# Queries, keys and their stacks made and loaded by halves of the tokens

## Chip, cores and metric

One core of one Trainium2 chip runs the whole program. The metric is the device time of one execution in microseconds (us), as a median over several executions. The chip has one tensor engine (TensorE, PE in the profile; its weight loads stand apart as PEld), a vector engine (VectorE, DVE), a scalar engine (ScalarE, ACT), GpSimd (POOL) and a queue engine (SyncE, SP) that issues nearly all transfers. 16 DMA engines move the data.

## The reference

The input is `x`, 16 images of 192 channels and 32 x 32 pixels. Two layers follow each other:

```python
x = _L0_conv_ref(x, ...)     # norm, q/k/v by 1x1 and 3x3 convolutions, attention over channels, + norm
t = _to_tokens(x)            # 1024 tokens of 192 channels in each image
t = t + _L1_attn_ref(_ln_t(t), W_qkv, W_proj, b_proj)   # 6 heads of 32, causal
t = t + _L1_ffn_ref(_ln_t(t), gate_w, gate_b, w1, b1, w2, b2)   # 4 experts, the best 2 for each token
```

The change lies in the causal token attention:

```python
qkv = jnp.einsum('btc,fc->btf', x, W_qkv)
wei = jnp.einsum('bqhd,bkhd->bhqk', q, k) * scale
wei = jnp.where(causal[None, None], wei, -jnp.inf)
out = jnp.einsum('bhqk,bkhd->bqhd', jax.nn.softmax(wei, axis=-1), v)
```

A query sees only keys that stand at or before it. Queries 0 to 511 so need only keys 0 to 511.

## The kernel before

The program goes through the 16 images one after another (about 171 us each), and then through 67 blocks of 512 routed tokens for the experts. All order is written out by hand: each engine has one list of instructions, and semaphores tie the lists together. A wait holds up everything behind it on its engine.

**The stages of an image.** Convolutions and channel attention come first, then the input of the token attention (`t_sb`, normed to `xhat`). TensorE transposes `xhat` (`norm_transposes`, one call for tokens 0 to 511 and one for the others). ScalarE and VectorE split each transposed half into a high and a low part (`T0`, `T1`, `T2`). `queries_keys(i, n)` then makes 128 rows (32 queries and 32 keys for each of two heads) for one half of the tokens. `f` in `QK_ORDER` is the pair of heads and the second number is the half. There are six such products of five matmuls. ScalarE copies each to `QKh`, and VectorE writes what is left to `QKl`. `values_of_tokens` makes the values.

**The stacks.** A score in near full precision needs three products. Therefore SyncE copies queries and keys inside SBUF into `QS` and `KS`, with 96 rows for each head: high, low, high queries against high, high, low keys. `load_queries` and `load_keys` issue three transfers each. The two heads of pair 0 come first (12 transfers of 128 KB, semaphores `stack_ld[0]` and `[1]`), the four other heads then (12 of 256 KB, `stack_ld[2]` and `[3]`). `QS` lies over `xhat` and over `xhat2`, the rows that GpSimd sends to the experts for the image before. Hence the second set waits for `sent`.

**Units.** The attention of an image has 48 units, `SOFT`: query chunks `qc` of 128 queries by head `h`, chunk by chunk. A unit is a score (`query_scores`), its maximum (VectorE), the exponential (ScalarE), the transposes of the weights (`blocks`), their copy to `PT` (ScalarE or VectorE), and the product with the values once four or two heads are there. Scores run two or three units ahead. `PT` lies over `QKh` and `QKl`, so the first copies of an image wait for all of `stack_ld`.

**What else hangs on SyncE.** Right behind the stacks, SyncE issues the load of the next image (`load_image`, `x_sb`, 768 KB) and zeros for the next expert blocks. VectorE reads that `x_sb` in the middle of the attention: `image_steps` puts `stats(i + 1, 0)` (L803) right behind the copies of unit 6, with a wait for `x_ld`. The further statistics and the norm of the next image follow at fixed units up to unit 27. In the last image, the expert weights (`w_raw`) are loaded in place of the next image, and VectorE splits them from unit 20 on (`split`, L1231 and L1232).

**GpSimd** sends the rows of the image before with 16 indirect transfers (`send`), in two sets of 8, with the two small `token_rstd` between them. It then adds a bias to `t_sb` (L732).

Of the kernel before, what the change touches and what calls it, by code (L numbers as in the profile page):

```python
# [5 lines left out]
F32 = mybir.dt.float32  # L6
# [10 lines left out]
BANK = 512  # L17

def hybrid_block_kernel(nc, x, ln_g, ln_b, conv_w, conv_bias_row, conv_taps, conv_bias, alpha_rows, w_f_t, b_f,  # L20
                        w_qkv_a, w_qkv_b, w_proj, w_proj_t, b_proj, gate_w_a, gate_w_b, gate_b, w1_a, w1_b, b1_t,
                        w2, b2, out):
    B, C, SH, SW = x.shape
    N = SH * SW
    NC = N // P
# [46 lines left out]
    with ExitStack() as ctx:  # L72
# [203 lines left out]
        ring_ld = [sem(f"ring_ld{p}") for p in range(PAIRS)]  # L276
        stack_ld = [sem(f"stack_ld{n}") for n in range(4)]
        x_ld, scr_w, t_st, sent, cleared, dram_written = sems("x_ld scr_w t_st sent cleared dram_written")
# [144 lines left out]

        QK_ORDER = [(0, 0), (1, 0), (0, 1), (2, 0), (1, 1), (2, 1)]
        NQ = len(QK_ORDER)
        QK_FIRST = 1
        COUNT_BANK = 7
# [32 lines left out]
        def _(sp):  # L460
# [64 lines left out]
            for i in range(B):  # L525
                if i:

                    sp.wait_ge(o_sb, NC * i)
                    sp.dma_start(tokens[i - 1], t_sb[:, :, 0:C]).then_inc(t_st, 16)
                def load_queries(j, first, end, signal):  # L530

                    for r, part in enumerate((QKh, QKl, QKh)):
                        sp.dma_start(QS[D * r:D * (r + 1), 2 * first + j:2 * end:2, :].bitcast(F32),
                                      part[D * j:D * (j + 1), first:end, :].bitcast(F32)).then_inc(signal, 16)

                def load_keys(j, first, end, signal):
                    for r, part in enumerate((QKh, QKh, QKl)):
                        sp.dma_start(KS[D * r:D * (r + 1), 2 * first + j:2 * end:2, :].bitcast(F32),
                                      part[64 + D * j:64 + D * (j + 1), first:end, :].bitcast(F32)).then_inc(signal, 16)  # L540

                sp.wait_ge(qk_lo, NQ * i + QK_ORDER.index((0, 1)) + 1)
                for j in range(2):
                    load_queries(j, 0, 1, stack_ld[j])
                    load_keys(j, 0, 1, stack_ld[j])
                sp.wait_ge(qk_lo, NQ * (i + 1))
                if i:

                    sp.wait_ge(sent, SENT * i)
                for j in range(2):  # L550
                    load_queries(j, 1, PAIR_GROUPS, stack_ld[2 + j])
                    load_keys(j, 1, PAIR_GROUPS, stack_ld[2 + j])
                if i + 1 < B:
# [74 lines left out]
        def _(pool):  # L628
# [93 lines left out]
            for i in range(B):  # L722
                unpad_image(pool, i)
                if i:
                    send(i - 1, 0, TPC)
                token_rstd(i, 0)
                token_rstd(i, 1)
                if i:
                    send(i - 1, TPC, NC)

# [9 lines left out]
                token_rstd2(i, 1)  # L740
            send(B - 1, 0, TPC)
            send(B - 1, TPC, NC)

# [46 lines left out]
        def _(dve):  # L790
# [182 lines left out]
            def blocks_out(i, n):  # L973

                qc, h = SOFT[n]
                for t in passage(i).of[n]:
                    eng, count, k0, nb = passage(i).pieces[t]
                    if eng == "dve":
                        dve.wait_ge(pT_ps, blocks_before(i, t))
                        if qc:  # L980
                            dve.wait_ge(pv_ps, 2 * (NC * i + qc - 1) + (1 if h < 4 else 2))
                        elif h == 1:
                            for signal in stack_ld:
                                dve.wait_ge(signal, STACK_LOADS * (i + 1))
# [355 lines left out]
        def _(act):  # L1340
# [48 lines left out]
            def blocks_out(i, n):  # L1389

                qc, h = SOFT[n]
                for t in passage(i).of[n]:
                    eng, count, k0, nb = passage(i).pieces[t]
                    if eng == "act":
                        act.wait_ge(pT_ps, blocks_before(i, t))
                        if qc:
                            act.wait_ge(pv_ps, 2 * (NC * i + qc - 1) + (1 if h < 4 else 2))
                        elif h == 0:
                            for signal in stack_ld:
                                act.wait_ge(signal, STACK_LOADS * (i + 1))  # L1400
# [91 lines left out]
        def _(pe):  # L1492
# [143 lines left out]
            def query_scores(i, n):  # L1636
                qc, h = SOFT[n]
                if n == 0:
                    pe.wait_ge(qk_lo, NQ * (i + 1))
                if n < H:  # L1640
                    pe.wait_ge(stack_ld[h if h < 2 else 2 + h % 2], STACK_LOADS * (i + 1))
                if last_user(n) is not None:
                    pe.wait_ge(exp_sb, NU * i + last_user(n) + 1)
# [299 lines left out]
```

## Time and profile before

| | us |
|---|---|
| median of 3 runs | 4002.49 (3996.62 to 4022.53) |
| the profiled execution, time | 3976.27 |
| its span | 3974.5 |
| TensorE busy | 3252.2 (82%) |
| VectorE busy | 2360.8 (59%) |
| ScalarE busy | 1836.1 (46%) |
| GpSimd busy | 1076.2 (27%) |
| TensorE clock, mean share of full speed | 0.906 |

All durations below come from the profiled execution. Busy shares are means over stages with different limits. So they are read by stage. A row of a timeline gives the start, the duration, the engine and the line of the code, then what was written and read. In square brackets it gives how long the engine stood idle before the row, and what ended that. "SPq" is the issue of a transfer, not the transfer.

### The profile page before, as it was taken

What the parts mean: (1) busy time and instruction counts of PE and PEld (TensorE: products, weight loads), DVE (VectorE), ACT (ScalarE), POOL (GpSimd) and SP (SyncE); (2) the same over time, 40 slices, a digit from 0 to 9 for tenths busy, and PEclk for the clock granted to TensorE, in tenths of its full rate; (3) what the DMA queues carried; (4) which work ended last, traced back from release to release, by engine and by line L of the source; (5) the groups of instructions that cost most, each with busy time, mean ns of one, the idle gap of its engine ahead of it and who ended that gap; (6) DMA issues with size and microseconds to landing.
All of it is one profiled execution on the core that took longest, in us unless ns stands there. A gap on an engine that the chain in (4) does not pass through costs nothing. (4 is left out here: it accounts for less than half of the span.)

```text
span 3974.5 us, 72989 instructions
## 1 busy us (share of the span) xinstructions
PE 3252.2 (82%) x26642; PEld 2468.7 (62%) x26642; DVE 2360.8 (59%) x5963; ACT 1836.1 (46%) x3868; POOL 1076.2 (27%) x1542
## 2 busy tenths in 40 slices
PE   3687887878779787787978779787499999999995
PEld 1465565565545555565565556555488888888884
DVE  3466565666647566465666647566456565656664
ACT  0345263543625435263543526445355555555553
POOL 1011202112020211202112020211336555565543
PEclk9898898988889898898988879897799999999998
DMA  6344353443533335343443533334123433333332
GB/s 148 97 102 122 96 136 89 101 107 87 145 106 94 97 93 132 96 123 92 102 107 88 147 101 94 93 97 116 46 71 106 118 99 109 99 114 94 117 104 86
DMA packets 213097, 414.47 MB, mean 104 GB/s; under 512 B 66799, under 2 KB 130223, under 8 KB 211673
## 3 DMA queue, kind: packets, MB, share of 16 engines
q1 hardware_dynamic: 188169, 359.44, 34.3%
q0 software_dynamic: 24576, 50.36, 4.2%
q8 instruction: 217, 3.56, 0.4%
q14 instruction: 135, 1.11, 0.1%
HBM read 242.86 MB, written 117.71 MB: 91 GB/s over the span
## 5 line engine op out<-in xcount | busy, mean ns | idle before, releaser
L971 DVE TENSOR_REDUCE minus_max<-ps 128x1 f32<-128x128 f32 (+7 forms) x768 | 575.9, 750 | 514.8 <-PE ps L1649 510.0
L1647 PE MATMUL ps<-KS,QS 96*128 96x512 f32 (+3 forms) x1152 | 433.0, 430 | 295.8 <-DMA KS<-QKl 260.1
L1386 ACT ACTIVATE p_sb<-ps,minus_max 128x128 f32<-128x128 f32 (+7 forms) x768 | 567.7, 741 | 115.5 <-DVE minus_max L971 112.0
L1659 PE MATMUL ps<-ident,p_sb 128*128 128x128 f32 x3456 | 555.2, 286 | 31.1 <-ACT p_sb L1386 7.8
L1401 ACT ACTIVATE PT<-ps 128x512 f32<-128x512 f32 (+3 forms) x640 | 340.6, 532 | 395.4 <-PE ps L1659 388.6
L1273 DVE TENSOR_TENSOR g_lo<-g,g_hi 128x512 fp32r<-128x512 f32 x402 | 315.4, 786 | 348.5 <-ACT g_hi L1476 296.9
L1475 ACT ACTIVATE g<-ps,bcur 128x512 f32<-128x512 f32 x402 | 276.6, 688 | 474.3 <-PE ps L1837 373.0
L1853 PE MATMUL ps<-w_all,g_hi 128*128 x1608 | 442.1, 355 | 18.2 <-ACT g_hi L1476 9.2
L706 POOL COPY inverse_wide<-inverse_sums 128x192 f32<-128x192 f32 x128 | 44.7, 349 | 1484.5 <-DVE inverse_sums L993 1484.5
L1647 PEld LDWEIGHTS ps<-KS,QS 96*128 96x128 f32 x1152 | 217.6, 212 | 357.1 <-DMA KS<-QKl 265.7
L1659 PEld LDWEIGHTS ps<-ident,p_sb 128*128 128x128 f32 x3456 | 385.1, 146 | 79.3 <-issue 33.3
L1530 PE MATMUL ps<-ring,wconv 125*32 125x512 f32 (+1 forms) x3072 | 375.2, 630 | 56.7 <-DMA ring<-padded_scratch 56.7
L719 POOL DMA_INDIRECT routed_rows<-xhat,slot x256 | 250.3, 978 | 414.5 <-issue 414.5
L756 POOL CAST cur<-w_all 128x384 fp32r x536 | 289.5, 586 | 244.1 <-PE ps L1837 244.0
L774 POOL DMA_INDIRECT got<-expert_rows,slot x256 | 259.5, 1014 | 201.5 <-issue 133.9
L1858 PE MATMUL ps<-w_all,g_lo 128*128 x1608 | 298.8, 267 | 14.8 <-DVE g_lo L1273 14.3
L1858 PEld LDWEIGHTS ps<-w_all,g_lo 128*128 128x128 f32 x1608 | 288.2, 189 | 29.0 <-DVE g_lo L1273 26.4
L1853 PEld LDWEIGHTS ps<-w_all,g_hi 128*128 128x128 f32 x1608 | 264.9, 192 | 50.7 <-issue 16.7
L985 DVE COPY PT<-ps 128x512 f32<-128x512 f32 (+3 forms) x512 | 246.4, 481 | 71.6 <-PE ps L1659 71.5
L1476 ACT ACTIVATE g_hi<-ps,bcur 128x512 fp32r<-128x512 f32 x402 | 273.7, 681 | 0.0
L1837 PE MATMUL ps<-X_hi,cur 128*128 128x512 f32 x804 | 263.6, 409 | 1.5 <-DVE X L1282 1.5
L1530 PEld LDWEIGHTS ps<-ring,wconv 125*32 125x32 f32 (+1 forms) x3072 | 97.3, 115 | 262.5 <-issue 249.2
(277 smaller groups left out, 5924.4 us busy)
## 6 DMA issues: line engine op xcount, KB each, us to landing
ring<-padded_scratch SPq DMA_DIRECT2D x576, 204.0 KB
routed_rows<-zero_rows SPq DMA_DIRECT2D x67, 384.0 KB, 6.9
xgt<-routed_rows SPq DMA_DIRECT2D x67, 384.0 KB
expert_rows<-y_rows SPq DMA_DIRECT2D x67, 384.0 KB, 2.5
QS<-QKh SPq DMA_DIRECT2D x64, 256.0 KB, 4.6
KS<-QKh SPq DMA_DIRECT2D x64, 256.0 KB, 5.0
padded_scratch<-xpad SPq DMA_DIRECT2D x16, 870.0 KB, 4.6
x_sb<-x SPq DMA_DIRECT2D x16, 768.0 KB, 7.6
```

Of the source, the lines that this page charges most:

```text
L756: g.tensor_copy(cur[r % 2][:, part], w_all[:, bass.ds(expert, 1), part].rearrange("p e f -> p (e f)")).then_inc(cur_sb, 1)
L971: v.tensor_reduce(nmx[:, qc, h:h + 1], score_place(n), AX, ALU.max, negate=True).then_inc(mx_sb, 1)
L1273: v.tensor_tensor(g_lo[:, n % 2, :], g32[:, n % 2, :], g_hi[:, n % 2, :].bitcast(F32), ALU.subtract).then_inc(lo_sb, 1)
L1386: a.activation(p_sb[n % NP][:, 0:P * (qc + 1)], score_place(n), ACT.Exp, bias=nmx[:, qc, h:h + 1], accum_out=ls[:, qc, h:h + 1]).then_inc( ...
L1401: a.activation(PT[h][:, k0:k0 + nb, :], bank(pass_bank(t))[:, 0:P * nb].rearrange("p (k q) -> p k q", q=P), ACT.Copy).then_inc(PT_act, 1)
L1475: a.activation(g32[:, n % 2, :], bank(n % 2), ACT.Gelu, bias=b1)
L1476: a.activation(g_hi[:, n % 2, :], bank(n % 2), ACT.Gelu, bias=b1).then_inc(gelu_sb, 1)
L1530: last = t.matmul(bank(2 * (r % 2) + nh)[W * j:W * (j + 1), :], wconv[s][0:KROWS[s], h, c0:c0 + W], rhs, start=s == 0, stop=s == 1, skip_g ...
L1647: t.matmul(o[:, k0:k0 + keys], QS[0:96, h, P * qc:P * (qc + 1)], KS[0:96, h, k0:k0 + keys], start=True, stop=k0 + keys < P * (qc + 1), ski ...
L1659: last = t.transpose(bank(pass_bank(piece))[:, P * k:P * (k + 1)], p_sb[n % NP][:, P * (k0 + k):P * (k0 + k + 1)], ident[:, :])
L1853: t.matmul(bank(acc_bank(r, tt))[:, 0:2 * C], g_hi[:, n % 2, P * tt:P * (tt + 1)], w2j, start=j == 0, stop=False, skip_group_check=True)
L1858: last = t.matmul(bank(acc_bank(r, tt))[:, 0:C], g_lo[:, n % 2, P * tt:P * (tt + 1)], w2j[:, 0:C], start=False, stop=j == J - 1, skip_grou ...
```

## The change

`QK_ORDER` now makes all three pairs of heads for tokens 0 to 511, then all for the others, and the second transposes stand behind the first three products (`QK_FIRST` is 3). The stacks are loaded in the same order, in 36 transfers where there were 24, with the same bytes in all. There are 12 of 64 KB (pair 0, first half), 12 of 128 KB (the four other heads, first half; keys first), and 12 of 192 KB (all heads, second half). Rows inside a transfer are 2 KB long where they were 4 KB. Two new semaphores, `stack_ld[4]` and `[5]`, tell of the second half. They are waited for at query chunk 4. GpSimd sends 12 transfers ahead of the two `token_rstd` and 4 behind them, where it was 8 and 8.

```diff
-        QK_ORDER = [(0, 0), (1, 0), (0, 1), (2, 0), (1, 1), (2, 1)]
+        QK_ORDER = [(0, 0), (1, 0), (2, 0), (0, 1), (1, 1), (2, 1)]
-        QK_FIRST = 1
+        QK_FIRST = PAIR_GROUPS
...
-                sp.wait_ge(qk_lo, NQ * i + QK_ORDER.index((0, 1)) + 1)
+                sp.wait_ge(qk_lo, NQ * i + 1)
+                sp.wait_ge(lnT_ps, 4 * (i + 1))
                 for j in range(2):
-                    load_queries(j, 0, 1, stack_ld[j])
-                    load_keys(j, 0, 1, stack_ld[j])
-                sp.wait_ge(qk_lo, NQ * (i + 1))
+                    load_queries(j, 0, 1, 0, stack_ld[j])
+                    load_keys(j, 0, 1, 0, stack_ld[j])
+                sp.wait_ge(qk_lo, NQ * i + PAIR_GROUPS)
+                for j in range(2):
+                    load_keys(j, 1, PAIR_GROUPS, 0, stack_ld[2 + j])
                 if i:
 
                     sp.wait_ge(sent, SENT * i)
                 for j in range(2):
-                    load_queries(j, 1, PAIR_GROUPS, stack_ld[2 + j])
-                    load_keys(j, 1, PAIR_GROUPS, stack_ld[2 + j])
+                    load_queries(j, 1, PAIR_GROUPS, 0, stack_ld[2 + j])
+                sp.wait_ge(qk_lo, NQ * (i + 1))
+                for j in range(2):
+                    load_queries(j, 0, PAIR_GROUPS, 1, stack_ld[4 + j])
+                    load_keys(j, 0, PAIR_GROUPS, 1, stack_ld[4 + j])
                 if i + 1 < B:
                     load_image(sp, i + 1)
...
-                    send(i - 1, 0, TPC)
+                    send(i - 1, 0, 6)
...
-                    send(i - 1, TPC, NC)
+                    send(i - 1, 6, NC)
...
-                            for signal in stack_ld:
+                            for signal in stack_ld[0:4]:
+                                dve.wait_ge(signal, STACK_LOADS * (i + 1))
+                        if qc == TPC and h == 0:
+                            for signal in stack_ld[4:6]:
                                 dve.wait_ge(signal, STACK_LOADS * (i + 1))
...
-                if n < H:
+                if qc == 0:
                     pe.wait_ge(stack_ld[h if h < 2 else 2 + h % 2], STACK_LOADS * (i + 1))
+                if qc == TPC and h < 2:
+                    pe.wait_ge(stack_ld[4 + h], STACK_LOADS * (i + 1))
```

**TensorE, between the first product of queries and keys and the first that needs the second half of the tokens.** L1593 (L1602 after) are the transposes of `xhat`. Before:

```order
L1609 MATMUL ps<-T_128,wqkv_b_hi 128x512
L1609 MATMUL ps<-T_128,wqkv_b_lo 128x512
L1593 MATMUL ps<-ident,xhat 128x128 [waits xhat_sb]
L1593 MATMUL ps<-ident,xhat 128x128 x7
L1609 MATMUL ps<-T_hi,wqkv_a_hi 128x512
L1609 MATMUL ps<-T_hi,wqkv_a_lo 128x512
L1609 MATMUL ps<-T_lo,wqkv_a_hi 128x512
L1609 MATMUL ps<-T_128,wqkv_b_hi 128x512
L1609 MATMUL ps<-T_128,wqkv_b_lo 128x512
L1609 MATMUL ps<-T_hi,wqkv_a_hi 128x512 [waits T_hi,T_lo]
```

Now:

```order
L1618 MATMUL ps<-T_128,wqkv_b_hi 128x512
L1618 MATMUL ps<-T_128,wqkv_b_lo 128x512
L1618 MATMUL ps<-T_hi,wqkv_a_hi 128x512
L1618 MATMUL ps<-T_hi,wqkv_a_lo 128x512
L1618 MATMUL ps<-T_lo,wqkv_a_hi 128x512
L1618 MATMUL ps<-T_128,wqkv_b_hi 128x512
L1618 MATMUL ps<-T_128,wqkv_b_lo 128x512
L1602 MATMUL ps<-ident,xhat 128x128 [waits xhat_sb]
L1602 MATMUL ps<-ident,xhat 128x128 x7
L1618 MATMUL ps<-T_hi,wqkv_a_hi 128x512 [waits T_hi,T_lo]
```

The second transposes have moved behind two more products (ten matmuls), and the product that waits for the second half comes right behind them, where one product stood between.

**SyncE, the end of the stack loads and what follows them.** `QS` are the stacked queries, `KS` the stacked keys, the sizes are rows x heads x tokens. Before:

```order
L534 DMA QS<-QKh 32x2x1024
L534 DMA QS<-QKl 32x2x1024
L534 DMA QS<-QKh 32x2x1024
L539 DMA KS<-QKh 32x2x1024 x2
L539 DMA KS<-QKl 32x2x1024
L316 DMA x_sb<-x 96x2x1024 [waits conv_ps]
L333 DMA routed_rows<-zero_rows 16x6144 x4
```

Now:

```order
L533 DMA QS<-QKh 32x3x512 [waits qk_lo]
L533 DMA QS<-QKl 32x3x512
L533 DMA QS<-QKh 32x3x512
L539 DMA KS<-QKh 32x3x512 x2
L539 DMA KS<-QKl 32x3x512
L533 DMA QS<-QKh 32x3x512
L533 DMA QS<-QKl 32x3x512
L533 DMA QS<-QKh 32x3x512
L539 DMA KS<-QKh 32x3x512 x2
L539 DMA KS<-QKl 32x3x512
L316 DMA x_sb<-x 96x2x1024 [waits conv_ps]
L333 DMA routed_rows<-zero_rows 16x6144 x4
```

The last 12 transfers now carry the second half of all six heads. The load of `x_sb` still stands behind all of them, and there are now 36 issues ahead of it since the products, where there were 24.

**GpSimd, the sends of the image before.** Before:

```order
L719 DMA routed_rows<-xhat_136,slot 34304x192 [waits cleared,slot_sb,xhat2_sb]
L719 DMA routed_rows<-xhat_136,slot 34304x192 x7
L694 TENSOR_TENSOR rstd<-rstd,minus_half 128x4 [waits veps] x2
L719 DMA routed_rows<-xhat_136,slot 34304x192 [waits xhat2_sb]
L719 DMA routed_rows<-xhat_136,slot 34304x192 x7
L732 TENSOR_TENSOR t_sb<-t_sb,bproj_bc 128x1568 [waits xhat_sb]
```

Now:

```order
L726 DMA routed_rows<-xhat_136,slot 34304x192 [waits cleared,slot_sb,xhat2_sb]
L726 DMA routed_rows<-xhat_136,slot 34304x192 x11
L701 TENSOR_TENSOR rstd<-rstd,minus_half 128x4 [waits veps] x2
L726 DMA routed_rows<-xhat_136,slot 34304x192 [waits xhat2_sb]
L726 DMA routed_rows<-xhat_136,slot 34304x192 x3
L739 TENSOR_TENSOR t_sb<-t_sb,bproj_bc 128x1568 [waits xhat_sb]
```

Four of the sends have moved ahead of the two `rstd` rows.

## Rows read from the trace of the kernel before

**Rows 1.** Windows: length, busy us (count) of each engine, clock, DMA share, GB/s

```profile
990.50:1014.70 24.20, 8.03 (x57) 7.08 (x55) 2.96 (x7) 5.10 (x15) 5.49 (x3) 0.68 0.90 219
1014.70:1020.20 5.50, 5.48 (x33) 4.26 (x34) 2.98 (x11) 3.46 (x17) 0.00 (x0) 0.53 1.00 364
1020.20:1039.00 18.80, 16.57 (x158) 11.61 (x156) 16.33 (x42) 13.80 (x44) 2.10 (x7) 1.00 0.02 7
```

**Rows 2.** Page, costliest groups: busy, mean ns | idle before, what ended it

```profile
L1647 PE MATMUL ps<-KS,QS 96*128 96x512 f32 (+3 forms) x1152 | 433.0, 430 | 295.8 <-DMA KS<-QKl 260.1
```

**Rows 3.** Timeline, PE: start us, us, operation [idle before <-what ended it]

```profile
1000.06 0.48 PE L1647 MATMUL ps<-KS,QS 96*128 96x128 f32 x1 [2.75 <-DMA KS<-QKl]
...
1007.98 0.47 PE L1647 MATMUL ps<-KS,QS 96*128 96x128 f32 x1 [7.31 <-DMA KS<-QKl]
...
1014.70 0.47 PE L1647 MATMUL ps<-KS,QS 96*128 96x128 f32 x1 [6.12 <-DMA KS<-QKl]
...
1038.94 0.60 PE L1647 MATMUL ps<-KS,QS 96*128 96x512 f32 x2
```

**Rows 4.** Timeline, SP: issues of the sixth image

```profile
990.53 0.54 SPq L534 DMA_DIRECT2D QS<-QKh  x1
...
998.40 0.63 SPq L534 DMA_DIRECT2D QS<-QKh  x1
999.07 0.62 SPq L534 DMA_DIRECT2D QS<-QKl  x1
...
1010.02 0.63 SPq L539 DMA_DIRECT2D KS<-QKl  x1
1010.69 1.21 SPq L316 DMA_DIRECT2D x_sb<-x  x1
```

**Rows 5.** Windows: the DMA share and rate while the stacks are loaded

```profile
1000.00:1005.00 5.00, 0.60 (x2) 0.42 (x2) 0.29 (x1) 0.46 (x2) 0.00 (x0) 0.50 1.00 216
```

**Rows 6.** DMA view, 980:1020 us: KB each, median us to landing

```profile
x_sb<-x SPq DMA_DIRECT2D x1, 768.0 KB, 7.8
QS<-QKh SPq DMA_DIRECT2D x4, 128.0 KB, 2.7
```

**Rows 7.** Timeline, DVE: where the next image's x is first read

```profile
1020.07 0.18 DVE L993 RECIPROCAL inverse_sums<-row_sums 128x6 f32<-128x6 f32 x1
1020.17 0.65 DVE L803 BATCH_NORM_STATS2 pstat<-x_sb 96x6 f32<-96x512 f32 x1
```

**Rows 8.** Line view of L316: who waited for x (us, times)

```profile
  DVE pstat L803: 7.1, 1
```

**Rows 9.** Timeline, PE: first product, second transposes, full-clock matmuls

```profile
981.97 0.80 PE L1609 MATMUL ps<-T_hi,wqkv_a_hi 128*128 128x512 f32 x1 [1.42 <-DVE T L952]
...
984.47 1.68 PE L1593 MATMUL ps<-ident,xhat 128*128 128x128 f32 x8
...
986.45 0.40 PE L1609 MATMUL ps<-T_lo,wqkv_a_hi 128*128 128x512 f32 x1
986.68 0.40 PE L1609 MATMUL ps<-T,wqkv_b_hi 128*128 128x512 f32 x1
```

**Rows 10.** Windows: the clock after 985 us

```profile
985.00:990.00 5.00, 4.59 (x22) 3.65 (x21) 2.96 (x5) 2.46 (x5) 2.59 (x3) 0.93 0.17 59
```

**Rows 11.** Timeline, POOL: last send of the first set, first rstd, the addition

```profile
961.15 0.97 POOL L719 DMA_INDIRECT routed_rows<-xhat,slot  x1 [0.31 <-issue]
974.31 1.04 POOL L694 TENSOR_TENSOR rstd<-rstd,minus_half 128x4 f32<-128x4 f32 x1 [12.19 <-DVE rstd L935]
...
992.86 3.56 POOL L732 TENSOR_TENSOR t_sb<-t_sb,bproj_bc 128x1568 f32<-128x1568 f32 x1
```

**Rows 12.** Timeline, DVE: first use of the expert weights in the last image

```profile
2737.14 0.55 DVE L1231 CAST w_all<-w_raw 128x768 fp32r<-128x768 f32 x1
```

**Rows 13.** Tile view of w_raw: last four loads, landing min/median/max

```profile
L563 SPq DMA_DIRECT2D w_raw<-w x4: 1052/3020/4105, 2713.7 to 2722.1; - x4
...
DMA to landing us min/median/max: 9.5/11.4/12.9
```

More of the change, by code:

```diff
@@ L276, in hybrid_block_kernel @@
         ring_ld = [sem(f"ring_ld{p}") for p in range(PAIRS)]
-        stack_ld = [sem(f"stack_ld{n}") for n in range(4)]
+        stack_ld = [sem(f"stack_ld{n}") for n in range(6)]
         x_ld, scr_w, t_st, sent, cleared, dram_written = sems("x_ld scr_w t_st sent cleared dram_written")
@@ L529, in _, with load_queries, load_keys @@
                     sp.dma_start(tokens[i - 1], t_sb[:, :, 0:C]).then_inc(t_st, 16)
-                def load_queries(j, first, end, signal):
+                def load_queries(j, first, end, half, signal):
+                    cols = slice(BANK * half, BANK * (half + 1))
                     for r, part in enumerate((QKh, QKl, QKh)):
-                        sp.dma_start(QS[D * r:D * (r + 1), 2 * first + j:2 * end:2, :].bitcast(F32),
-                                      part[D * j:D * (j + 1), first:end, :].bitcast(F32)).then_inc(signal, 16)
-                def load_keys(j, first, end, signal):
+                        sp.dma_start(QS[D * r:D * (r + 1), 2 * first + j:2 * end:2, cols].bitcast(F32),
+                                      part[D * j:D * (j + 1), first:end, cols].bitcast(F32)).then_inc(signal, 16)
+                def load_keys(j, first, end, half, signal):
+                    cols = slice(BANK * half, BANK * (half + 1))
                     for r, part in enumerate((QKh, QKh, QKl)):
-                        sp.dma_start(KS[D * r:D * (r + 1), 2 * first + j:2 * end:2, :].bitcast(F32),
-                                      part[64 + D * j:64 + D * (j + 1), first:end, :].bitcast(F32)).then_inc(signal, 16)
-                sp.wait_ge(qk_lo, NQ * i + QK_ORDER.index((0, 1)) + 1)
+                        sp.dma_start(KS[D * r:D * (r + 1), 2 * first + j:2 * end:2, cols].bitcast(F32),
+                                      part[64 + D * j:64 + D * (j + 1), first:end, cols].bitcast(F32)).then_inc(signal, 16)
+                sp.wait_ge(qk_lo, NQ * i + 1)
+                sp.wait_ge(lnT_ps, 4 * (i + 1))
                 for j in range(2):
-                    load_queries(j, 0, 1, stack_ld[j])
-                    load_keys(j, 0, 1, stack_ld[j])
-                sp.wait_ge(qk_lo, NQ * (i + 1))
+                    load_queries(j, 0, 1, 0, stack_ld[j])
[3 more added lines that the diff above has]
+                    load_keys(j, 1, PAIR_GROUPS, 0, stack_ld[2 + j])
                 if i:
@@ L740, in _ @@
                 token_rstd2(i, 1)
[L741 to L742 removed]
+            send(B - 1, 0, NC)
             pool.wait_ge(w_split, 1)
@@ L1398, in blocks_out @@
                         elif h == 0:
-                            for signal in stack_ld:
+                            for signal in stack_ld[0:4]:
                                 act.wait_ge(signal, STACK_LOADS * (i + 1))
```

## The prediction

> **What bounds the kernel now.** I read the page first, for the waits that cost the bound engine most. TensorE stood idle for 260.1 us before score matmuls until a transfer to `KS` had landed [rows 2], about 16 us in each of 16 images. Then I took one image, the sixth, by its timelines. Its first unit to need the last stack starts at 1014.70 us, after waits of 2.75, 7.31 and 6.12 us for stacks [rows 3]. From the first stack issue at 990.53 [rows 4] to that start, 24.2 us go by in which TensorE is busy for 8.0 [rows 1]. The last stack alone sets this end. The first copies to `PT` wait for all stacks, so nothing past three units can flow before.
>
> The wait is one for bandwidth. While the stacks load, the 16 DMA engines are busy for 1.00 of the time at 216 GB/s [rows 5]. The four other heads' first stack was complete at 1007.98 and the second, six transfers of 256 KB later, at 1014.70 [rows 3]. That is 6.72 / 6 = 1.12 us for each, or 234 GB/s.
>
> What is next in line decides this case. Behind the stacks SyncE issues the next image's `x_sb`, at 1010.69 [rows 4], and it lands 7.8 us later [rows 6], at 1018.5. It comes 3.8 us behind the last stack. VectorE reads it at 1020.17, straight after other work [rows 7]. So x has 1.7 us to spare. In all images the only wait for x is the first image's, 7.1 us [rows 8]. This place in VectorE's list is 5.5 us behind the start of the units (1014.70 to 1020.17). If the units start over 1.7 us earlier and x does not, VectorE stops there with the scores' maxima and copies queued behind it. ScalarE and TensorE then stop within about three units.
>
> **The change, part by part.** *Start of the loads.* They now wait for the second transposes, since `QS` lies over `xhat`. The first product starts at 981.97 and the transposes at 984.47, so five matmuls take 2.5 us at half clock. At full clock one matmul takes 986.68 - 986.45 = 0.23 us [rows 9]. The window from 985 has a mean clock of 0.93 [rows 10]: 0.7 us at half, so the clock rises at 985.7. Of the ten matmuls that now come first, 2.7 fit into the 1.2 us from 984.47 to 985.7, at 0.46. The other 7.3 take 1.7 us. The transposes then start at 987.4. They took 1.68 us at half clock [rows 9], and I give them 0.9. The loads start at 988.3, 2.2 us before the old 990.53.
>
> *First half.* The old first 12 issues took 998.40 - 990.53 = 7.87 us, or 0.66 each. The next, with twice the rows, came 0.67 apart at first (998.40, 999.07) [rows 4]. An issue so has a cost of its own, and a transfer of 64 KB does not fill it (128 KB took 0.56 by the rate above). Hence 12 x 0.66 + 12 x 0.67 = 15.9 us, to 1004.2. The last issue before that lands after 2.7 us [rows 6], at about 1006.5. The units start 8.2 us earlier than now. By itself this is the gain: 8.2 us an image.
>
> *Second half.* 12 transfers of 192 KB at 0.75 x 1.12 = 0.84 us are 10.1 us. Before, the last stack landed at 1014.70 where 998.40 + 12 x 1.12 gives 1011.8, so 2.9 us of latency come on top. The new last stack lands at 1004.2 + 10.1 + 2.9 = 1017.2. Chunk 4 needs it about 24 us after the start of the units (before, 1014.70 to 1038.94 [rows 3]), so at 1030. It is hidden, by 13 us.
>
> *The next image's x.* It moves with the queue: 1017.2 + 3.8 = 1021.0, against 1018.5. The bytes ahead of it are unchanged. They start 2.2 us earlier, but 12 issues of 64 KB leave the engines half idle, and the 128 KB ones a little, for about 12 x 0.38 + 12 x 0.11 = 5.9 us, of which the old start-up already had 12 x 0.10 = 1.2. VectorE, which would be there at 1012.0, waits 9 us and starts at 1021.0 where it started at 1020.17: 0.8 us later.
>
> *After that wait.* Two effects. TensorE and ScalarE are about two units ahead. VectorE is the busiest from 1020.2 on after TensorE, 16.33 of 18.8 us [rows 1], so such a lead can win at most its 2.5 us of idle time. I give it 1.0. Against this, TensorE starts again at half clock. After the old stop the clock stood at 0.53 over 5.5 us and was full after that [rows 1]. In 1020.2:1039 TensorE is busy for 16.57 of 18.8 us at the full clock, so 3 to 5 us at half clock in it can cost from nothing (work done ahead) to 2.5. I take 1.0, the nearer end since scores three units ahead are made. The sum is nothing, between -2.5 and +2.5.
>
> *GpSimd.* Its first 8 sends end at 962.1, and the first `rstd` is released at 974.31 by VectorE after 12.19 us of idling [rows 11]. Four more at 1.28 (0.97 and 0.31 idle) take 5 us of that: no cost. `sent` comes 5 us earlier, but was not waited for. The addition to `t_sb` (3.56 us) moves ahead too and is hidden by 24 us. If that cover were gone it would cost its length at most.
>
> *Two more waits on TensorE.* The product for the second half comes right behind the transposes and waits for both splits. As for the first half, this costs up to 1.42 us [rows 9]. The stacks' wait hides it.
>
> *The last image.* It has no x, but the expert weights are next. The last of these loads is issued at 2722.1 and lands 9.5 us later [rows 13], at 2731.6. VectorE begins with them at 2737.14 [rows 12]. Now it would be there at 2729.0, and the weights land 2.5 us later than before, at 2734.1. Gain: 3.0 us.
>
> **The sum.** 15 x 0.8 - 3.0 = +9 us on the profiled 3976.3, so 3985. That execution is 26 us (0.7%) below the median of the three runs, 4002.5. The forecast for the median is 4002.5 + 9 = 4011: no measurable difference (a measurement of this kernel can tell about 1%, 40 us, from no change).
>
> **The rivals.** *The gain survives in part.* If x lands sooner than I say, the stop is shorter. If short issues cost less than 0.66, or the second half flows better, the bytes could be through as early as the start moved: x at 1018.5 - 2.2 = 1016.3, VectorE 3.9 us earlier, 15 x -3.9 - 5 = -63, so 3939. For it: the engines have reached more than 234 GB/s on other transfers (364 in 1014.7:1020.2 [rows 1]). Against it: 0.66 for each issue even where 0.56 of data was waiting. The whole 8.2 (3876) would need x at 1012, so 3.1 MB of second half and x within 8 us of 1004.2, where I count 17. Chance of faster by over 1%: 0.13.
>
> *Slower: the second half runs at the pace of its rows, not its bytes.* The new transfers have 96 rows of 2 KB, where the old ones had 64 of 4 KB. If a row costs 60% of an old one and not 50%, 12 transfers take 12.1 us, x lands at 1023.0, and the sum is 15 x 2.8 - 1 = +41: 4043, where the case decides. If each takes as long as an old issue under pressure, 1.25 us, then 15.0 us, x at 1025.9, 15 x 5.7 + 2 = +88: 4090. For it: the rate of short rows inside SBUF is not in the trace. Against it: the DMA engines, not the issues, were the limit for 64 rows. A second way to the same side is a restart at the dear end of my bounds, +2.5 an image. Chance of slower by over 1%: 0.27.
>
> *The order of products costs something itself*, in that TensorE reaches the first score later, by 1 to 1.5 us (1.42 at most for the wait, as above). The stack and x waits behind it are longer than that, so it does not show.
>
> **How the numbers follow.** Forecast (the stop for x eats the gain, within 1%): 0.60, with its own range of 3965 to 4043. Faster 0.13, slower 0.27. The range of 3965 to 4065 leaves about 0.12 below and 0.08 above.
>
> **What would show it.** In an image like the sixth: a first stack issue 2 us earlier, TensorE's third and fourth waits for `KS` down to a start of the units 8 us earlier, and a new wait of VectorE at L803 for x, some 9 us in each of 15 images. The clock falls a second time there. x lands about 33 us after the first stack issue (28.0 before). VectorE's first wait in the last image is at its split. I am wrong if L803 does not wait, or if the time from its start to the end of the image changes by over 2.5 us.

## The result and the profile after

The changed kernel takes 4025.36 us (median of 4 runs, 4019.5 to 4028.73). The kernel before took 4001.7 us beside it (4 runs). The ratio is 1.0052, with a 95% interval of 1.0027 to 1.0077: within 1%, as forecast, and 14 us above the 4011 predicted. A second comparison, at another time, gave 1.0034 (1.0016 to 1.0053).

The profiled execution took 4019.5 us (span 4017.8, mean clock 0.907). Its page has the row that answers to [rows 2]:

```profile
L1658 PE MATMUL ps<-KS,QS 96*128 96x512 f32 (+3 forms) x1152 | 437.4, 435 | 143.2 <-DMA QS<-QKh 103.6
```

TensorE waits 103.6 us for stacks where it waited 260.1. So 156 us of wait are gone, and the kernel is not faster. I follow the sixth image again. TensorE's timeline (start us, us, operation, idle before and what ended it) has the products, then the three waits for stacks:

```profile
990.00 0.79 PE L1618 MATMUL ps<-T_hi,wqkv_a_hi 128*128 128x512 f32 x1 [1.42 <-DVE T L958]
...
995.47 1.04 PE L1602 MATMUL ps<-ident,xhat 128*128 128x128 f32 x8
998.37 0.50 PE L1618 MATMUL ps<-T_hi,wqkv_a_hi 128*128 128x512 f32 x1 [1.86 <-DVE T L958]
...
1007.14 0.33 PE L1658 MATMUL ps<-KS,QS 96*128 96x128 f32 x1 [0.46 <-DMA KS<-QKl]
...
1012.66 0.48 PE L1658 MATMUL ps<-KS,QS 96*128 96x128 f32 x1 [5.12 <-DMA QS<-QKh]
...
1014.54 0.47 PE L1658 MATMUL ps<-KS,QS 96*128 96x128 f32 x1 [1.27 <-DMA QS<-QKh]
```

SyncE's timeline has the issues of the stacks, and of x behind them:

```profile
996.58 0.55 SPq L533 DMA_DIRECT2D QS<-QKh  x1
...
1003.50 0.59 SPq L539 DMA_DIRECT2D KS<-QKl  x1
1004.14 2.23 SPq L539 DMA_DIRECT2D KS<-QKh  x2
...
1012.19 1.25 SPq L533 DMA_DIRECT2D QS<-QKh  x2
...
1021.81 0.61 SPq L539 DMA_DIRECT2D KS<-QKl  x1
1022.46 0.60 SPq L316 DMA_DIRECT2D x_sb<-x  x1
```

The sixth image is now 8 us later in the program, for reasons told below, so I count from its first product, 981.97 before [rows 9] and 990.00 now. The first stack issue comes at +6.58 (before +8.56, [rows 4]), right behind the second transposes (they end at 996.51), for which it waits. The units flow from +24.54 (1014.54; before 1014.70, +32.73, [rows 3]): 8.2 us earlier. The load of x is issued at +32.46 (before +28.72). The windows (length, busy us of PE, PEld, DVE, ACT and POOL, clock, DMA share, GB/s) of the first half's loads, and of the stretch in which 192 KB transfers take over, stand against 1.00 and 216 in [rows 5]:

```profile
996.60:1014.50 17.90, 9.32 (x61) 8.23 (x61) 4.63 (x9) 5.94 (x17) 2.95 (x1) 0.91 0.61 142
1014.70:1019.70 5.00, 4.98 (x31) 3.80 (x31) 2.63 (x9) 3.35 (x16) 0.00 (x0) 0.50 0.97 213
```

The queue runs at 142 GB/s while it issues small transfers, and at 213 once they are of 192 KB. The DMA view (KB each, median us to landing):

```profile
KS<-QKh SPq DMA_DIRECT2D x4, 192.0 KB, 3.9
x_sb<-x SPq DMA_DIRECT2D x1, 768.0 KB, 6.5
...
QS<-QKh SPq DMA_DIRECT2D x4, 64.0 KB, 2.0
```

Then VectorE's timeline, where it comes to the next image's x, and the line view of that load (who waited, us and times; landing):

```profile
1019.92 0.18 DVE L1002 RECIPROCAL inverse_sums<-row_sums 128x6 f32<-128x6 f32 x1
1029.00 0.69 DVE L809 BATCH_NORM_STATS2 pstat<-x_sb 96x6 f32<-96x512 f32 x1 [8.90 <-DMA x_sb<-x]
```

```profile
  DVE pstat L809: 146.1, 16
...
DMA to landing us min/median/max: 6.3/6.6/7.4
```

The reading of x begins at +39.00, where it was at +38.20 [rows 7]. VectorE is ready for it at +30.10, 8.1 us earlier than it was, and stands there for 8.90 us. Over the kernel that is 146.1 us in 16 waits, where there was one of 7.1 [rows 8]. Of the 156 us that left TensorE's wait for stacks, 139 came back as VectorE's wait for x.

The stretch after that, by windows, against the third row of [rows 1]:

```profile
1019.90:1029.00 9.10, 3.26 (x17) 1.98 (x15) 0.20 (x3) 2.00 (x7) 0.52 (x2) 0.50 1.02 287
1029.00:1038.50 9.50, 8.01 (x40) 4.97 (x40) 7.05 (x19) 3.94 (x13) 0.53 (x2) 0.50 0.22 91
1038.50:1050.03 11.53, 10.12 (x103) 7.52 (x103) 9.24 (x24) 8.31 (x26) 1.06 (x3) 1.00 0.01 3
```

During the stop the clock is at 0.50 (1.2 GHz). It stays there for 9.5 us more, although TensorE is busy for 8.01 of them, and only then is it full (2.4 GHz). In this image it had been at 0.50 since the waits for stacks: it is so in 1014.70:1019.70 too, with TensorE busy for 4.98 of 5.00 us. In 12 of the 15 images it came back once between the two stops and fell again, and in 3, of which the sixth is one, it did not. And last, the tile view of the expert weights in the last image, where no x is loaded:

```profile
L1240 DVE CAST w_all<-w_raw x12: 516/559/751, 2752.1 to 2783.8; 128x768 fp32r<-128x768 f32 x8, 128x1152 fp32r<-128x1152 f32 x4
...
  DVE w_all L1240: 6.1, 1
```

To see all images and not one, I read these points out of the timelines of the first 15 images and took means (us). "Read of x" is the start of the first statistics, "stop" the idle time right before it, "chunk 4" the 25th unit, "rest" the time from the last unit to the next image's first product. A unit is taken here at its mask matmul (L1649, L1660 after), the last of its score, 0.3 to 0.6 us behind the start of the unit.

| kernel | first product to first stack issue | first stack issue to fourth unit | first product to read of x | stop | read of x to chunk 4 | chunk 4 to last unit | rest | image |
|---|---|---|---|---|---|---|---|---|
| before | 8.29 | 24.65 | 38.13 | 0 | 19.77 | 45.02 | 66.95 | 169.88 |
| after | 6.21 | 17.83 | 38.39 | 9.27 | 21.32 | 44.52 | 66.71 | 170.94 |

An image is 1.06 us longer: +0.26 to the read of x, +1.55 from there to chunk 4, -0.50 and -0.24 behind that. Fifteen of them are +15.9, and the last image is about 2.5 us shorter. The fourth unit comes 8.9 us earlier on the mean (6.21 + 17.83 against 8.29 + 24.65). The sixth image is no mean one: it is 3.8 us longer than before.

### The profile page after: what moved, and what is told of

Same layout as the page of the kernel before. It is cut to its first block and busy times, and to the rows that moved or that the text cites. A ratio compares the mean times of both kernels' runs of the same rounds, so it can differ in the third digit from the quotient of the medians.

```text
span 4017.8 us, 73230 instructions
## 1 busy us (share of the span) xinstructions
PE 3280.6 (82%) x26642; PEld 2487.5 (62%) x26642; DVE 2378.1 (59%) x5963; ACT 1841.2 (46%) x3868; POOL 1065.5 (27%) x1542
## 5 line engine op out<-in xcount | busy, mean ns | idle before, releaser
L1670 PE MATMUL ps<-ident,p_sb 128*128 128x128 f32 x3456 | 569.0, 291 | 164.3 <-DVE PT L994 135.4
L1658 PE MATMUL ps<-KS,QS 96*128 96x512 f32 (+3 forms) x1152 | 437.4, 435 | 143.2 <-DMA QS<-QKh 103.6
L1282 DVE TENSOR_TENSOR g_lo<-g,g_hi 128x512 fp32r<-128x512 f32 x402 | 338.6, 844 | 354.7 <-ACT g_hi L1485 275.7
L1670 PEld LDWEIGHTS ps<-ident,p_sb 128*128 128x128 f32 x3456 | 393.2, 149 | 211.9 <-issue 163.6
L1539 PE MATMUL ps<-ring,wconv 125*32 125x512 f32 (+1 forms) x3072 | 365.9, 616 | 60.2 <-DMA ring<-padded_scratch 60.2
L762 POOL CAST cur<-w_all 128x384 fp32r x536 | 275.6, 562 | 287.3 <-PE ps L1848 287.2
```

The costliest lines, as they stand in the source:

```text
L1282: v.tensor_tensor(g_lo[:, n % 2, :], g32[:, n % 2, :], g_hi[:, n % 2, :].bitcast(F32), ALU.subtract).then_inc(lo_sb, 1)
L1539: last = t.matmul(bank(2 * (r % 2) + nh)[W * j:W * (j + 1), :], wconv[s][0:KROWS[s], h, c0:c0 + W], rhs, start=s == 0, stop=s == 1, skip_g ...
L1658: t.matmul(o[:, k0:k0 + keys], QS[0:96, h, P * qc:P * (qc + 1)], KS[0:96, h, k0:k0 + keys], start=True, stop=k0 + keys < P * (qc + 1), ski ...
L1670: last = t.transpose(bank(pass_bank(piece))[:, P * k:P * (k + 1)], p_sb[n % NP][:, P * (k0 + k):P * (k0 + k + 1)], ident[:, :])
```

## The experiments

The runs were made in four sittings, and times differ by 3% between them: the kernel before took 4001.7 us beside the first result, 3888.8 and 3887.1 us in the next two sittings, and 4003.8 in the last. So every ratio is to the kernel before in the same sitting, and stages are compared within one, unless it is said.

### Both kernels again

The kernel before, unchanged:

> The kernel before, unchanged, for a second trace. In the first pair of traces the 16 images account for +15 us of the change (1.6 to the first product, 15 x 1.06, then -2.6 in the last image) and the expert stage, whose code is the same, for +28 us (1116.7 to 1144.7 from its first matmul to the end). If the expert stage merely varies from execution to execution, this trace has an expert stage of a length unlike 1116.7, nearer to 1140, with image stages of 169.9 us as before. If the change lengthens the expert stage, it is again within 3 us of 1116.7.

And the changed kernel, unchanged:

> The changed kernel, unchanged, timed again on the chip of these runs. Theory (the image stages carry the change, and the expert stage does not): the images cost 1 us each more than before, 15 x 1.06 + 1.6 - 2.6 = +15 us, so a ratio near 1.004, and an expert stage of the same length as that of the other kernels on the same chip. Rival (the change lengthens the expert stage by its own): a ratio of 1.010 or more.

The kernel before took 3881.84 us in one run (13 others: 3888.84). The changed kernel took 3898.69, ratio 1.0034 (1.0016 to 1.0053). The first pair of traces differ by 43 us of span, of which 15 come from the images (+15.9, -2.5 in the last, and a first product 1.6 us later). The rest, +28, is in the stage of the experts behind the last image: 1116.7 us before, 1144.7 after. In the second pair this stage takes 1067.4 us in both, the spans differ by 16.3 (3880.1 and 3896.4), and the image by 1.39 (166.81 and 168.20). So the change does not lengthen the experts' stage. I had expected a stage nearer to 1140 us and images of 169.9 in the second trace of the kernel before: both were shorter. Most of the +28 lies in one operation. By line (count | busy, mean ns | idle before), the changed kernel and the kernel before, both of the first pair:

```profile
L1282 DVE TENSOR_TENSOR g_lo<-g,g_hi 128x512 fp32r<-128x512 f32 x402 | 338.6, 844 | 354.7 <-ACT g_hi L1485 275.7
```

```profile
L1273 DVE TENSOR_TENSOR g_lo<-g,g_hi 128x512 fp32r<-128x512 f32 x402 | 315.4, 786 | 348.5 <-ACT g_hi L1476 296.9
```

The busy time differs by 23 us. The median of one is 693 ns in both, but 19 take over 1 us in one and 8 in the other, up to 4 us. In the second pair it is busy for 302.3 and 302.4 us. The effect of the change alone is thus +13 to +16 us.

### x ahead of the stacks

SyncE issues the load of the next image's x ahead of the stacks, right behind the store of the image before. This is done in the changed kernel and in the kernel before (the line numbers differ):

```diff
+                if i + 1 < B:
+                    load_image(sp, i + 1)
                 ...
                     load_keys(j, 0, PAIR_GROUPS, 1, stack_ld[4 + j])
                 if i + 1 < B:
-                    load_image(sp, i + 1)
                     clear_blocks(sp, i + 1)
```

> The changed kernel with one move: the load of the next image's x is issued ahead of the stacks. Theory (the stop for x at L809 and the restart after it eat the gain): no wait of VectorE for x, units still start 24.0 us after the first product, the first read of x 29.3 us after it (38.4 in the changed kernel, 38.1 before), and from there to query chunk 4 about 19.8 us and not 21.3. Each image 9.3 + 1.6 = 10.8 us shorter than in the changed kernel, 160.1 us: 15 x 10.8 = 162 us, near 3865. Rival (the transfers of the second half, or VectorE's own work, hold the units up anyway): chunk 4 stays where it is, and the time stays within 30 us of 4025.

> The kernel before with the same move of the load of x. Theory (x had 1.7 us to spare there and set nothing): within 10 us of the kernel before, 3992 to 4012. Rival (the early x helps in itself, for example by leaving the queue free): faster by 30 us or more.

With the change: 3760.59 us, ratio 0.9673 (0.9641 to 0.9704). Without: 3887.04, 0.9986 (0.9965 to 1.0007). The change with x ahead of it, SyncE's timeline and VectorE's:

```profile
904.78 0.33 SPq L316 DMA_DIRECT2D x_sb<-x  x1
936.22 0.55 SPq L536 DMA_DIRECT2D QS<-QKh  x1
```

```profile
959.55 0.18 DVE L1004 RECIPROCAL inverse_sums<-row_sums 128x6 f32<-128x6 f32 x1
959.65 0.65 DVE L811 BATCH_NORM_STATS2 pstat<-x_sb 96x6 f32<-96x512 f32 x1
```

x is issued 31 us before the first stack, and VectorE goes on to it without a stop. Who waited for it, over the whole kernel, there and in the kernel before with x first:

```profile
  DVE pstat L811: 7.1, 1
```

```profile
  DVE pstat L805: 7.0, 1
```

Only the first image waits. The means of the image are 159.10 us against 168.20 (changed) and 166.81 (before); the read of x is at 29.55 us from the first product, where it was at 38.59. So the change has its gain of 8 us an image as soon as x isn't queued behind it. The early x by itself gives nothing, since x was not waited for before the change. The stage from the read of x to chunk 4 falls from 21.33 to 19.91 with the stop, but the rest of the image grows by 1.43 (63.72 to 65.15), so the image is 9.1 us shorter and not the 10.8 that I expected. In that rest TensorE has the half clock for 11.7 us on the mean and not 8.6, and is busy for 55.0 us and not 53.8. It also waits 0.8 us longer for `xhat`. Why the clock falls for longer there is open.

### The reading of x later

VectorE's list reads x behind units 6, 8 and 10. It is moved to where the data have nearly come:

```diff
-                image_steps = {6: lambda: stats(i + 1, 0), 8: lambda: stats(i + 1, 1), 10: lambda: stats(i + 1, 2),
+                image_steps = {9: lambda: stats(i + 1, 0), 10: lambda: stats(i + 1, 1), 11: lambda: stats(i + 1, 2),
```

> The changed kernel with the first three statistics of x moved from VectorE's places 6, 8 and 10 to 9, 10 and 11; loads and all else as in the changed kernel. Theory (the place in VectorE's list sets what waits for x): x lands at the same time, about 38.4 us after the first product, but units 7 to 9 are done by then, so the stop is about 3.3 us shorter and as much of the image is behind it: 15 x 3 = 45 us less than the changed kernel, ratio 0.988 to the changed kernel. Rival (VectorE waits, but TensorE or the DMA sets the pace): within 10 us of the changed kernel.

It took 3855.7 us, ratio 0.9912 (0.9878 to 0.9945), or 0.988 of the changed kernel. x comes no sooner (first product to read of x 38.45, before the edit 38.59), but three units more lie ahead of the wait, which is 6.27 us and not 9.36:

```profile
  DVE pstat L809: 101.0, 16
```

The image has 165.08 us, 3.12 less, which is the 3.09 that left the stop. So it is the place of the wait in VectorE's list that costs, and each microsecond of it counts in full.

### The short transfers made longer

The first half's 24 transfers of 64 and 128 KB become 12 of 192 KB, behind the third product (the waits of the other engines for `stack_ld` follow suit and are not shown):

```diff
-                sp.wait_ge(qk_lo, NQ * i + 1)
-                sp.wait_ge(lnT_ps, 4 * (i + 1))
-                for j in range(2):
-                    load_queries(j, 0, 1, 0, stack_ld[j])
-                    load_keys(j, 0, 1, 0, stack_ld[j])
                 sp.wait_ge(qk_lo, NQ * i + PAIR_GROUPS)
+                sp.wait_ge(lnT_ps, 4 * (i + 1))
                 for j in range(2):
-                    load_keys(j, 1, PAIR_GROUPS, 0, stack_ld[2 + j])
+                    load_keys(j, 0, PAIR_GROUPS, 0, stack_ld[j])
                 ...
                 for j in range(2):
-                    load_queries(j, 1, PAIR_GROUPS, 0, stack_ld[2 + j])
+                    load_queries(j, 0, PAIR_GROUPS, 0, stack_ld[j])
```

> The changed kernel with its first half of the stacks in 12 transfers of 192 KB (all six heads, keys first) in place of 24 of 64 and 128 KB. x stays behind the stacks. Theory (the issue time of short transfers delays the units and x): first issue about 7.0 us after the first product, units at 20.5 us (24.0 in the changed kernel), x read at 33.4 (38.4), still with a wait of VectorE of about 7.5 us and a slow restart of 21.3 us to chunk 4. 5.0 us an image: about 3950. Rival (the DMA engines are the limit whatever the cut): x read within 1 us of 38.4, and the time within 15 us of 4025.

It took 3847.81 us, ratio 0.9897 (0.9868 to 0.9927). SyncE's timeline (the first product of this image starts at 952.59) and the window of the first half's loads:

```profile
959.07 1.26 SPq L539 DMA_DIRECT2D KS<-QKh  x2
...
971.40 0.95 SPq L533 DMA_DIRECT2D QS<-QKh  x1
...
980.24 0.81 SPq L316 DMA_DIRECT2D x_sb<-x  x1
```

```profile
960.00:972.00 12.00, 8.48 (x57) 7.62 (x57) 2.74 (x5) 4.83 (x13) 2.41 (x1) 1.00 0.91 201
```

The DMA engines are at 0.91 and 201 GB/s, against 0.61 and 142. The issue of x comes at +27.65, where it was at +32.46 with 24 short issues (means +27.8 and +31.7 within the sitting). VectorE's stop is not much shorter, since the units begin earlier too:

```profile
987.16 0.69 DVE L805 BATCH_NORM_STATS2 pstat<-x_sb 96x6 f32<-96x512 f32 x1 [8.75 <-DMA x_sb<-x]
```

An image has 164.42 us, 3.8 less than the changed kernel (I had expected 5.0). The read of x is 4.1 us earlier (34.53 against 38.59), and all but 0.3 of it shows. This is the price of the short transfers, which the prediction had as a term of 5.9 us less the 1.2 that the old start had already.

### Both edits

x ahead of the stacks, and the long transfers, in one kernel:

> Both moves together: the first half of the stacks in 12 transfers of 192 KB, and x ahead of the stacks. Theory: no wait for x, units 20.5 us after the first product (24.0 with x first alone, 32.9 before), then 5.1 us to the read of x and 19.8 to chunk 4: 3.5 us an image less than with x first alone, whose ratio was 0.967. So 0.967 - 16 x 3.5 / 3889 = 0.953. Rival (something else, as the values or the first score, holds the units at about 24 us): ratio stays at 0.967.

It took 3707.66 us, ratio 0.954 (0.9509 to 0.957), the fastest of all. The image has 155.55 us, 3.55 less than with x ahead alone. The two gains add up.

### The order of the products alone

The kernel before with `QK_ORDER` and `QK_FIRST` of the change; the stacks are loaded as they were, by whole rows:

```diff
-        QK_ORDER = [(0, 0), (1, 0), (0, 1), (2, 0), (1, 1), (2, 1)]
+        QK_ORDER = [(0, 0), (1, 0), (2, 0), (0, 1), (1, 1), (2, 1)]
-        QK_FIRST = 1
+        QK_FIRST = PAIR_GROUPS
```

> The kernel before with the new order of products and transposes alone: all heads of the first half, then the second transposes, then the rest, and whole-token stacks as before. Pair 0 is complete only after the fourth product. Theory (the order costs, and only the loads by halves pay for it): the first stack is issued 11.0 us after the first product (8.3 before), units and x move with it, 2.7 us an image: +43, ratio 1.011. Rival (the order costs nothing in itself, since the products are the same): ratio 0.998 to 1.002.

It took 3915.29 us, ratio 1.0063 (1.0039 to 1.0086), +24 us. TensorE's timeline and SyncE's:

```profile
968.90 0.79 PE L1609 MATMUL ps<-T_hi,wqkv_a_hi 128*128 128x512 f32 x1 [1.70 <-DVE T L952]
...
973.82 1.04 PE L1593 MATMUL ps<-ident,xhat 128*128 128x128 f32 x8
976.72 0.50 PE L1609 MATMUL ps<-T_hi,wqkv_a_hi 128*128 128x512 f32 x1 [1.86 <-DVE T L952]
```

```profile
979.52 0.54 SPq L534 DMA_DIRECT2D QS<-QKh  x1
```

The second transposes start 4.9 us after the first product (2.5 before, [rows 9]), the product of the second half waits 1.86 us for its split, and the stacks start at +10.62 (+8.56 before). On the mean the stacks start 2.25 us later and x is read 2.05 later, of which 1.48 reach the image. I had expected 1.011. In the change the first half is loaded before the second is made, so the wait of 1.86 us for the split delays no load there. But the loads still wait for the second transposes, which the new order puts behind three products. In its sixth image the first pair's low part is written by 993.86, and the first stack issue comes at 996.58, when the transposes have ended (996.51). So by these rows up to 2.7 us of an earlier start are lost there, an estimate. No run moves the transposes alone.

### The sends alone

The kernel before with GpSimd's sends cut at 6 chunks and not at 4:

```diff
-                    send(i - 1, 0, TPC)
+                    send(i - 1, 0, 6)
                 ...
-                    send(i - 1, TPC, NC)
+                    send(i - 1, 6, NC)
```

> The kernel before with the sends split 12 and 4 where they were 8 and 8, alone. Theory (POOL has 12 us of idle time ahead of the first rstd, and nothing waits for the last send): ratio 0.998 to 1.002. Rival (the four sends delay the rstd, or the earlier addition to t_sb slows VectorE): 2 us an image or more, ratio 1.008.

It took 3998.88 us, ratio 0.9988 (0.9969 to 1.0008). GpSimd's timeline has the last of the first 12 sends and the first `rstd`, which had 12.19 us of idling ahead of it in [rows 11]:

```profile
965.23 0.96 POOL L719 DMA_INDIRECT routed_rows<-xhat,slot  x1 [0.30 <-issue]
973.19 1.04 POOL L694 TENSOR_TENSOR rstd<-rstd,minus_half 128x4 f32<-128x4 f32 x1 [7.00 <-DVE rstd L935]
```

Five of those 12 us are used and 7 are left. No cost of the sends shows, to 0.3%.

### The clock through the stop

In the changed kernel TensorE gets 38 matmuls of 512 columns with no use, whose product nobody reads, in the stretch where it waits for VectorE:

```diff
+                    if n == 9:
+                        for _ in range(38):
+                            t.matmul(bank(7), ident_r[:, :], wqa_hi[:, 0:BANK], start=True, stop=True, ...)
```

> The changed kernel with 38 matmuls of no use (128x512, into a bank that holds nothing at that time) ahead of the transposes of unit 9, where TensorE stands during the stop for x. They keep it busy for about 9 to 10 us and do nothing else. Theory (the 1.6 us by which the way from the read of x to chunk 4 is longer than before, 21.3 against 19.7, come from the half clock after the stop): the clock is full when x lands, the way is 19.7 or less, each image 1.6 us or more shorter, so 25 us less than the changed kernel: ratio 0.997 to the kernel before (the changed kernel's is 1.0034). If the lead of the other engines is worth its 1.0 us, up to 40 us less, 0.993. Rival (the clock costs nothing there, since VectorE sets the pace, and the longer way is the backlog of VectorE itself): ratio 1.003 or above.

It took 4004.92 us, ratio 1.001 (0.9988 to 1.0031); I had expected 0.997. TensorE's timeline, and the window of the 19.1 us that follow the read of x:

```profile
1024.07 8.91 PE L1782 MATMUL ps<-wqkv_a_hi,ident_r 128*128 128x512 f32 x38
```

```profile
1030.85:1049.94 19.09, 17.21 (x154) 12.40 (x152) 16.65 (x41) 12.62 (x38) 1.58 (x5) 1.00 0.11 45
```

The stop is as long as it was (9.27 us). The clock behind it is full all the way to chunk 4 in 12 of 15 images. On the mean it is at half for 0.7 us of that way, where it was for 9.2 in the changed kernel. From the read of x to chunk 4 it takes 19.49 us on the mean, where it took 21.33. The half clock behind the stop so costs 1.84 us an image, rather more than less: in the sixth image the added matmuls end (1032.98) 2.1 us behind the read of x, and in the changed kernel TensorE goes on after 1.5. Not all of it shows in the time. Chunk 4 to the last unit takes 0.6 us longer (45.10, where the changed kernel of the first sitting has 44.52), and in the last image, which has no stop, the 38 matmuls lie on the path: from the fourth unit to chunk 4 it takes 31.0 us and not 23.2, of which 6.3 come back in its wait for the weights. My expectation had left that image out. By these rows 15 x (1.84 - 0.58) - (7.8 - 6.3) = 17 us were to be won, 0.4%, from 1.0034 to 0.999. The measured 1.001 lies between the two, and its interval reaches nearly to both. So the ratio by itself doesn't tell them apart, and the cost of the clock rests on the stage.

The half clock also explains how the stage varies without any stop for x. Where the clock was full from the read of x to chunk 4, that way took 19.2 us on the mean in the kernel before (5 images of its trace) and 19.3 with the added matmuls (12 images).

## Why the prediction was right, and where it was not

The steps, from the first product of the sixth image, then on the mean:

| step | predicted | measured |
|---|---|---|
| first stack issue | +6.33 | +6.58 (mean +6.21) |
| issues of the first half | 15.9 | 16.3 |
| units start earlier by | 8.2 | 8.2 (mean 8.9) |
| last stack landed | +35.2 | about +35.7 (1021.81 + 3.9) |
| stop for x | 9 | 8.90 (mean 9.27) |
| read of x | +39.03 | +39.00 |
| later than before by | 0.8 | 0.8 (mean 0.26) |
| after the wait, to chunk 4 | | +2.3 (mean +1.55) |
| after the wait, to the end of the image | 0 (-2.5 to +2.5) | +3.0 (mean +0.8) |
| last image | -3.0 | -2.5 |

**Right, and shown.** The gain at the units is there (8.2 us in the sixth image, 8.9 on the mean), and it is lost at the wait for x at L809 (L803 before). That the position in the queue does it is shown from three sides: x ahead of the stacks brings the gain back (0.9673), the same move before the change brings nothing (0.9986), and reading x later brings back just what it takes from the wait (0.9912). The sum's two halves, an earlier start and more issues, are each measured: the split into short transfers costs 4.1 us of the read of x, where I had 4.7.

**The term that was mis-sized** is "After that wait. (...) The sum is nothing, between -2.5 and +2.5", with 1.0 for the lead and 1.0 for the clock. The lead of two units is worth about nothing: with the clock full all the way, the stretch took 19.3 us with it and 19.2 without. The clock costs 1.84. I had counted 3 to 5 us at half clock behind the wait. The old stop was my measure, after which the clock was full within 5.5 us of the start of the units. But that was the sixth image alone. On the mean of the 15 it took 7.0 us, so 1.7 us at half clock lay behind the read of x already before the change. Now it is 9.2 us on the mean (7.1 to 10.3). So 15 x 1.55 stands to chunk 4 where I had nothing: 23 us. Behind chunk 4 the image gives 11 of them back, for a reason not shown, and 12 are left of the term. That the read of x moved by 0.26 on the mean and not by 0.8 takes 8 us off. The sum is +15.9 from the images where I had 12. That it comes so near is in part luck, since these two misses are of opposite sign. My own sign of being wrong, a change of over 2.5 us from the read of x to the end of the image, shows in the sixth image (+3.0) and not on the mean (+0.8). The second fall of the clock is there in 12 images of 15, but not in the sixth. The sixth image spoke for the stop, but not for so small a difference as 0.8.

**The rest of the miss** (4025 against 4011) is most likely not the change's. Between the two first traces the experts' stage is 28 us longer, and in the second pair it is not. Only traced executions show this. What makes a few of its operations long is open.

**The rivals.** The gain surviving in part needed x 3.9 us earlier; it landed where forecast. Merging the transfers is what that rival had asked for, and it gives 0.9897, where its 3939 of 4002 is 0.984. The read of x is 3.7 us earlier than before the change (34.53 and 38.23), where that rival had 3.9. Slower by the pace of the rows does not occur: the new transfers of 96 rows of 2 KB run at 213 GB/s, the old at 216. The Trainium skill, SBUF — State Buffer, section "Door 1: The DMA port swizzle", has 8 of the 16 DMA ports for 32 partitions, by its port rate an estimate of 217 GB/s. The trace agrees within a few per cent, with 213 at a share of 0.97. On the mean of 14 images, the last set of stack loads ran at 226 GB/s in both kernels, with rows of 2 KB as with rows of 4 KB. No window of the stack loads came near the 435 GB/s that the Trainium skill, DMA: Bandwidth & Descriptors, section "Where 436 GB/s comes from", gives for transfers inside SBUF. The dear end of the restart was the part of that rival that came true in the sixth image (3.0 us, over its 2.5), but not on the mean (0.8). The order of the products costs 2.1 us of the read of x where the loads wait for both halves (1.0063). In the change TensorE's wait for the split is hidden, as forecast. What the order costs there lies in the start of the loads (+6.58), which the prediction had counted.

## What to carry to other kernels

When a wait for one transfer is shortened, ask what stands behind it in the same queue and who reads that: here the next load had 1.7 us to spare, and 8.2 us of gain turned into 9 us of waiting. Moving the load that has 30 us of free time ahead of the burst cost one edit and took the changed kernel from 1.003 to 0.967 of the kernel before. Without the change it gave nothing, so the two have to be tried together. Cutting a transfer to start earlier can lose more than it gains when the pieces take the DMA engines less time than their issue. Here 12 long transfers that waited for two more products let the fourth unit start 3.4 us earlier than 24 short ones (20.5 and 23.9 us behind the first product, on the mean).

One image is enough to find a stop of 9 us, but not to forecast a difference of 1 us. Such a term is better read as a mean over all images, the clock included.

## What the runs showed of the hardware

- **An issue has a fixed cost.** SyncE issues a transfer each 0.59 to 0.64 us, for 32 rows (64 KB) as for 64 and 96 rows of 2 KB when the DMA engines have room. At 64 KB that is 65,536 / 0.63 us = 104 GB/s, half of what the engines took at a share of 1.00. When the engines are behind, an issue takes longer: up to 1.17 us at 192 KB (changed kernel) and 1.39 at 256 KB (kernel before) in the sixth image.
- **Rows of 2 KB moved as fast as rows of 4 KB** inside SBUF: 213 GB/s at a share of 0.97, and 216 at 1.00. On the mean of 14 images it was 226 for both.
- **The clock came back late.** It stayed at 0.50 for 9.5 us with TensorE busy for 8.01 of them, and was full in the next 11.5 us with 10.12 busy. Ahead of that it was at 0.50 for 5 us with TensorE busy for 4.98. From the read of x it took 9.2 us on the mean of 15 images to be full, and 7.0 us from the start of the units in the kernel before. 38 matmuls of 512 columns during the stop kept it full. Each microsecond at half clock between the read of x and chunk 4 cost about 0.2 us (1.84 for 8.5).
- **The same kernel took 4002 or 3888 us**, by sitting. The two sittings at 3888 us were on chip 15 and the last, at 4004, on chip 12. Which chip the first was on is not on record, so it may be a difference between chips. Two places carry most of it. One is the experts' stage, with 1117 to 1145 us in the traces of the slower sittings and 1064 to 1083 in the others. The other is the rest of the image. There VectorE waits at L911 (L917 with the change) for something that the view finds nowhere in the trace and calls "remote" (us, times). All four traces of the slower sittings have it, with 50 to 56 us in 10 or 11 waits, and none of the eight others. The kernel before, line view of L911, in the first sitting and in the second:

```profile
  remote: 50.3, 10
  PE ps L1555: 36.3, 22
```

```profile
  PE ps L1555: 50.9, 32
```

What it waits for is open.
